# The order of work inside a step of the routed experts, on TensorE and on VectorE

## The reference, cut to what matters

```python
weights, indices = _gate(xt, gate_w)                 # 4 of 16 experts for each token
combine = jnp.einsum('tk,tke->te', weights, jax.nn.one_hot(indices, E, dtype=weights.dtype))
h1 = jnp.einsum('td,eid->tei', xt, W1)               # D = 256, inner width I = 176
h3 = jnp.einsum('td,eid->tei', xt, W3)
g = jax.nn.silu(h1) * h3 * combine[:, :, None]
y = jnp.einsum('tei,edi->td', g, W2)
```

## Time and profile before

| | us |
|---|---|
| median of 3 runs | 994.32 |
| the runs | 994.6, 990.09, 994.32 |
| the profiled execution | 992.58 |
| its span in the profile | 990.8 |

### The profile page before, as it was taken

One profiled execution on the slowest core, in us unless ns is written; L12 is line 12 of the kernel. 1 busy time (PEld: TensorE's weight loads), 2 busy tenths in 40 slices (PEclk: granted clock), 3 DMA queues, 4 the chain that ended last, 5 costly groups with the idle time before them and its releaser, 6 DMA issues.

```text
span 990.8 us, 19931 instructions
## 1 busy us (share of the span) xinstructions
PE 867.0 (88%) x6994; PEld 736.1 (74%) x6994; DVE 732.7 (74%) x1589; ACT 573.9 (58%) x1072; POOL 658.6 (66%) x625
## 2 busy tenths in 40 slices
PE   5688999999999999999999997738887899999940
PEld 5556777878878888788888786637775799999940
DVE  5777999987978788787888885585765466666648
ACT  1345777778887877887887886622321244444410
POOL 3555878978797888888788886515666555555530
PEclk9999999999999999999999999958997899999975
DMA  8661613223423235222325136233223333434337
GB/s 299 233 134 31 178 32 83 62 56 87 150 50 84 56 87 172 58 69 52 89 57 160 41 99 229 85 83 108 90 98 130 120 116 116 120 118 122 108 123 302
DMA packets 65757, 111.20 MB, mean 112 GB/s; under 512 B 16917, under 2 KB 43292, under 8 KB 63820
## 3 DMA queue, kind: packets, MB, share of 16 engines
q1 hardware_dynamic: 46905, 69.24, 26.4%
q10 hardware_dynamic: 11843, 22.84, 6.5%
q0 software_dynamic: 6912, 17.84, 4.9%
HBM read 46.06 MB, written 39.58 MB: 86 GB/s over the span
## 4 chain that ended last, share of the span: by engine, by line
PE 57%; DVE 11%; DMA 11%; POOL 11%; issue 5%; ACT 3%; SPq 0%; POOLq 0%; ACTq 0%; DVEq 0%
PE bank L691 12%; PE bank L693 10%; PE bank L692 10%; DMA slots<-h,slot_i 8%; PE bank L871 7%; PE bank L1087 7%; POOL p_lo L1927 5%; PE bank L848 4%; POOL turns L1905 2%; PE bank L1059 2%; PE bank L945 2%; DVE nmax L1261 2%; POOL slots L1983 1%; DVE qk L1241 1%; DVE turns L1235 1%
## 5 line engine op out<-in xcount | busy, mean ns | idle before, releaser
L1927 POOL TENSOR_TENSOR p_lo<-p_f,p_hi 128x512 f16<-128x512 f32 x256 | 329.5, 1299 | 46.2 <-ACT p_f L1662 45.2
L1659 ACT ACTIVATE p_hi<-bank,log_up 128x512 f16<-128x512 f32 x256 | 176.3, 689 | 108.0 <-PE bank L693 99.1
L1261 DVE TENSOR_REDUCE nmax<-bank 128x1 fp32r<-128x512 f32 x256 | 174.4, 685 | 84.4 <-PE bank L848 81.3
L1662 ACT ACTIVATE p_f<-bank,log_up 128x512 f32<-128x512 f32 x256 | 175.4, 685 | 14.7 <-POOL p_lo L1927 14.7
L871 PEld LDWEIGHTS bank<-vals,p_hi 128*128 128x128 f16 x2048 | 110.5, 98 | 59.2 <-POOL p_lo L1927 27.7
L871 PE MATMUL bank<-vals,p_hi 128*128 128x66 f16 x2048 | 138.8, 194 | 14.8 <-POOL p_lo L1927 14.5
L1905 POOL TENSOR_TENSOR turns<-turns 128x512 f32<-128x512 f32 x64 | 90.9, 1423 | 65.9 <-DVE turns L1235 65.9
L1241 DVE TENSOR_TENSOR qk<-rows_f,qk 128x512 fp32r<-128x512 f32 (+1 forms) x128 | 132.7, 1037 | 2.2
L691 PE MATMUL bank<-qk 128*128 128x512 f32 x256 | 122.2, 477 | 6.0 <-issue 4.8
L871 PE MATMUL bank<-vals,p_lo 128*128 128x66 f16 x1024 | 121.2, 193 | 0.0
L848 PE MATMUL bank<-qk 128*128 128x512 f32 x256 | 104.4, 411 | 3.6 <-DVE nmax L1261 3.2
(11 more groups left out here) (231 smaller groups left out, 2091.8 us busy)
## 6 DMA issues: line engine op xcount, KB each, us to landing
rows_f<-turns SPq DMA_DIRECT2D x64, 256.0 KB, 3.9
slots<-pad ACTq DMA_DIRECT2D x4, 2880.0 KB, 10.1
xs<-slots SPq DMA_DIRECT2D x80, 144.0 KB
w_hi<-parts SPq DMA_DIRECT2D x16, 512.0 KB, 8.4
rows_f<-kl_f SPq DMA_DIRECT2D x32, 192.0 KB, 3.0
w_raw<-in_w ACTq DMA_DIRECT2D x4, 1408.0 KB, 11.8
h_dram<-h_hl SPq DMA_DIRECT2D x3, 1024.0 KB, 4.9
qk<-lat_st SPq DMA_DIRECT2D x16, 192.0 KB, 4.3
```

What stands on the lines that cost most here:

```text
L1261: dve.tensor_reduce(nmax[:, k % MAXES:k % MAXES + 1], max_bank[q % 2][:], AX_X, ALU.max, negate=True)\
L1659: act.activation(p_hi[:, u % TB, :], score_bank[u % 2][:], ACT.Exp, bias=log_up[:, 0:1], scale=SCALE)
L1662: act.activation(p_f[:, u % 2, :], score_bank[u % 2][:], ACT.Exp, bias=log_up[:, 0:1], scale=SCALE)\
L1927: pool.tensor_tensor(p_lo[:, u % TB, :], p_f[:, u % 2, :], p_hi[:, u % TB, :], ALU.subtract).then_inc(s_pl, 1)
```

## The change

In TensorE's stream the transposes of tile n+3 move behind the first products of tile n+2. In VectorE's stream the copy to `gT` of tile n+1 moves ahead of the gated product and `sel_i` of tile n+2. No instruction is added or removed, and the semaphores that each waits for stay the same. ScalarE's, GpSimd's and SyncE's streams are unchanged.

```diff
@@ TensorE, expert_position @@
+                if within(n + 2, SLOT_TILES):
+                    m, par = n + 2, j % 2
+                    expert = experts[place + 2]
+                    pe.wait_ge(e_lo, m + 1)
...
+                    inner_products(par, par, ...).then_inc(e_h, 1)
                 if within(n + 3, SLOT_TILES):
...
                         mm = pe.transpose(x_bank[jm % 2][:, k * P:(k + 1) * P], xs[:, jm, k * P:(k + 1) * P], ident[:])
                     mm.then_inc(e_x, 1)
-                if within(n + 2, SLOT_TILES):
...
-                    inner_products(par, par, ...).then_inc(e_h, 1)
@@ VectorE, expert_position @@
+                if within(n + 1, SLOT_TILES):
...
+                    dve.tensor_copy(gT[:, par, 0].rearrange("p c t -> p (c t)"), g_bank[par][0:FC, 0:2 * P]).then_inc(e_gTc, 1)
                 if within(n + 2, SLOT_TILES):
...
                     dve.tensor_copy(sel_i[:, jm:jm + 1], sel[:, jm, 1:2]).then_inc(e_idx, 1)
-                if within(n + 1, SLOT_TILES):
...
-                    dve.tensor_copy(gT[:, par, 0].rearrange("p c t -> p (c t)"), g_bank[par][0:FC, 0:2 * P]).then_inc(e_gTc, 1)
```

More of the change, by code:

```diff
@@ L1050, in expert_position @@
                     place = j
+                if within(n + 2, SLOT_TILES):
+                    m, par = n + 2, j % 2
+                    expert = experts[place + 2]
+                    pe.wait_ge(e_lo, m + 1)
+                    if static(m) and m < 2:
+                        pe.wait_ge(z_g, 2 * NT)
+                    else:
+                        pe.wait_ge(e_g, m - 1)
+                    inner_products(par, par, lambda k: w_hi[:, bass.ds(expert, 1), k, :].rearrange("p a n -> p (a n)"),
+                                   lambda k: w_lo[:, bass.ds(expert, 1), k, :].rearrange("p a n -> p (a n)")).then_inc(e_h, 1)
                 if within(n + 3, SLOT_TILES):
@@ L1555, in expert_position @@
                     dve.tensor_reduce(sel[:, jm], chosen_by[:, jm], AX_X, ALU.add).then_inc(e_sel, 1)
+                if within(n + 1, SLOT_TILES):
+                    m, par = n + 1, (j + 1) % 2
+                    dve.wait_ge(e_gt, m + 1)
+                    if not (static(m) and m < 2):
+                        dve.wait_ge(e_y, m - 1)
+                    dve.tensor_copy(gT[:, par, 0].rearrange("p c t -> p (c t)"), g_bank[par][0:FC, 0:2 * P]).then_inc(e_gTc, 1)
                 if within(n + 2, SLOT_TILES):
```

## The result

| | before | after |
|---|---|---|
| median, us | 994.46 (6 runs) | 1011.75 (6 runs, 1009.74 to 1017.92) |
| profiled execution, us | 992.58 | 1009.74 |
| its span, us | 990.8 | 1007.9 |

The ratio of after to before is 1.0189, 95% interval 1.0165 to 1.0212. The changed kernel is slower by 17.3 us between the two medians, by about 19 us by the ratio (16 to 21 by its interval) and by 17.1 us between the two spans. The prediction was 1011.

A forecast was written before the change was run, and what follows sets the result against it. TensorE was taken to bound the routed experts' steps; a loop of 2.55 us replacing 2.268 gave +16.8 us, start's gain included, plus 1.0 for the low clock: +17.8, so 1010.4 or 1012.1, forecast 1011 us, range 1003 to 1025.

The forecast's parts named there:

- The loop and its length: Routed experts' steps: first products, next transposes, high half, low half, next first products close once a step, 2.55 us.
- 0.04: Loop term: from the transposes' end to the start of the high half on a free ScalarE, 0.04 us.
- 0.76: Loop term: from the low half's start to the first products that read it, 0.76 us, read at one place.
- The array's work: TensorE in the routed experts' steps needs 2.26 to 2.27 us a step of its own, whatever the order.
- VectorE's swap: Copy and gated product swapped on VectorE: nothing in the steady state; the start's gain alone would give -3.8 us.
- the low clock: After the start's idle time the clock is low and the loop longer there: +1.0 us, half of 2.
- The start: Tile 3's second products run in TensorE's idle time before 778.82; tile 6's products count from 779.1 us.
- the rival of the falling clock: Idle time of 0.28 us each step lowers the clock; such steps take 3.75 us, 1033 to about 1100; chance 0.08.
- The sequencer at every fourth step: Fetching the next tiles' experts every fourth step: put at 0; other end 0.2 us each time, 3.6 us, 1015.
- One sign: Middle steps: TensorE's busy share falls to about 89% at clock 1.00, about 0.28 us idle ahead of first product.

The follow-up runs named there:

- e4: Changed kernel with the next inputs' transposes moved behind those of the gated product, one place later still: 1026.59 us, 1.0333 of before, step 2.773 us.
- e6: Changed kernel with the high half copied in four activations of 64 columns instead of one of 256: 1023.53 us, 1.0307 of before, step 2.743 us.
- e3: Changed kernel with the two transposes put between the first three and last three first products: 991.12 us, 0.9983 of before, step 2.270 us.
- e5: Changed kernel with loads, transposes, high half and low half one tile further ahead: 991.20 us, 0.9970 of before, step 2.265 us.
- e2: Kernel before with VectorE's half of the change alone, TensorE in the old order: 990.18 us, 0.9969 of before, step 2.269 us.
- e1: Kernel before with TensorE's half of the change alone, VectorE in the old order: 1012.60 us, 1.0199 of before, step 2.555 us.
- e8: VectorE's half of the change alone, plus VectorE's conversion to `sel_i` two steps later, last in its step: 987.95 us, 0.9933 of before.

## Why the prediction was right

**The loop and its length: right, term by term.** The sum was 0.95 + 0.38 + 0.04 + 0.42 + 0.76 = 2.55. After reads 0.96 + 0.38 + 0.04 + 0.41 + 0.76 in the step shown, and 2.555 over 69 steps. The two terms that rested on the least held: 0.04, for which the row of a free ScalarE at the low clock was taken over the 0.09 of the steady step, and 0.76, which rested on one place. e4 and e6 show that the step follows the loop one for one (0.218 for 0.22, 0.188 for 0.19), e3 and e5 that it falls back to 2.27 as soon as the loop is shorter or spans another step.

**The array's work is the same in either order: right.** 2.265 to 2.270 in e2, e3 and e5, with three different orders.

**VectorE's swap costs nothing in the steady state and gains at the start: right, the gain smaller.** e2 shows both. Its gain is 3.1 us by the ratio and 1.4 in the traces, counted from the scatter's end (171.2 less 169.8). The forecast's own terms gave 3.8 for a kernel that has the start's gain and no loop, 2.8 with the low clock.

**The start: the mechanism right, its place in time off, the low clock too cheap.** The products of tile 6 were put at 779.1, 0.94 behind the conversion's start. After has them at 777.38 (the second one at 777.68, less the 0.30 spacing of the low clock), 0.99 behind the conversion at 776.39. What was off is the scatter's end itself, 1.8 us earlier than in the trace of before. The low clock was sized at +1.0, half of 2, because TensorE's idle time would be shorter; it was longer, 8.21 us. The low clock lasted from 777.23 to about 781.9 and cost 1.8: from 777.38 to the products of tile 79 at 965.67 it is 188.3, and 73 x 2.555 is 186.5. All of it falls in the first round, 4.37 us from the products of tile 6 to those of tile 7 (781.91 less 0.16). From the products of tile 79 on both kernels take the same, 42.2 and 42.3 us to the end of the span.

The price of such a round was also wrong in kind. The prediction took the loop at the low clock, 2.55 + 1.2 = 3.75, and so do the first steps of after, in which no second products run yet; they are 3.68 apart:

```profile
751.80 0.63 PE L1069 MATMUL bank<-ident,xs 128*128 128x128 f32 x2
...
755.48 0.63 PE L1069 MATMUL bank<-ident,xs 128*128 128x128 f32 x2
```

But in a full step at the low clock the array's own work is the longer one. In the old order, where nothing waits, such a step takes 4.33 (before, tiles 7 and 8):

```profile
780.67 0.64 PE L1059 MATMUL bank<-ident,xs 128*128 128x128 f32 x2
...
785.00 0.59 PE L1059 MATMUL bank<-ident,xs 128*128 128x128 f32 x2
```

So at that clock the new order costs next to nothing in a full step (4.37 and 4.33, one of each). A step of after at the low clock costs 1.8 over one at full clock, and not 1.2; the rival of the falling clock was priced a third too low.

**How near the number came is in part luck.** The products of tile 79 stand 17.15 us later than before (965.67 less 948.52). That is 73 x 0.287 = 20.95 for the longer steps, less 1.8 for the scatter's earlier end, less 2.0 for the rest of the start (the swap's gain and the low clock). The forecast had 20.6, nothing and 2.8 (3.8 less 1.0). The scatter's end moves from trace to trace and was not forecast; without it the difference of the two traces would have been 18.9.

**The sequencer at every fourth step: a few hundredths, not 0.2.** The idle time ahead of the waiting weight load runs 0.43, 0.43, 0.39, 0.45 and so on from step to step, with a pattern of four. All steps lie between 2.51 and 2.58.

**The clock: it stayed at 1.00.** The array stood for 0.28 us in each of 73 steps and the granted clock of 786 to 960 is 1.00. So the rule of the Trainium skill that the rival named ("TensorE: Matmul & The Clock Gate", "A second HAM failure mode: psum-queue depth-cycling") did not bite here, once the clock was full. In e4, with 0.5 us of standing time a step, the stretch from 800 to 940 us also has 1.00. These runs decide it, and not the shared expert's stretch, which the prediction held against the rival: its 0.94 hides two spells at 0.50, at its start and from 747 to 751, the second behind the 4.91 us shown above.

At the low clock the waits may matter, which the prediction did not have. The first steps of the routed experts run at 0.50 in every trace. In e2 the clock is at 0.50 from 750 to 755 and at 1.00 from 756 to 768. In after TensorE waits 1.09, 1.13 and 0.70 us at the head of the first three steps, and the clock stays low until about 761:

```profile
748.00:760.00 12.00, 8.95 (x31) 7.50 (x31) 2.91 (x14) 1.75 (x6) 7.67 (x9) 0.50 0.40 135
```

e1, e4 and e6 have such waits too and, like after, are low for about 14 us; the kernels with the short step, which wait less there, are low for about 7 (before for 3). That the waits held the clock down was not tested. Here it cost nothing, since TensorE stands for the scatter afterwards.

**One sign was wrong.** The prediction said that TensorE's busy share would fall to 89% in the profile. It reads 172.09 of 174, 99%. A matmul's row runs on for some time behind the point at which the next one could start (0.32 long, 0.16 apart), and these tails fill most of the standing time: in the step shown the second products' row ends at 863.36 (862.33 and 1.03), and the next first product's row starts at 863.39. So the idle time of 0.28 that the prediction looked for ahead of the first product cannot be read there either. It shows in the weight loads (0.43 ahead of L691) and in the number of matmuls in a microsecond, which fell to 89%. For the same reason the 160.00 of 160 us of the earlier trace rows did not by itself show that nothing waited before; what shows it is that the waits listed for that stretch of before have none of TensorE's weight loads among them.

## What to carry to other kernels

In a pipeline of steps that is bound by one engine, moving that engine's producer of a value from the front of a step to behind its consumer takes almost a step off the distance that hides the round trip. Before such a move, sum the round trip from start to start round the loop and compare it with the bound engine's own work in a step: the excess is paid each step (here to the hundredth of a microsecond), and a slack is worth nothing. A conversion that waits for a slow transfer should stand in its engine's queue as late as its reader allows, because all that stands behind it waits too.

## What the runs showed that had not been expected

- Standing time of the array hides in the busy share: 0.28 us of each 2.555 us step is 11%, and the profile's busy time shows 1%.
- From the low half's start to the weight load that waited for it, the traces of after and e1 show 0.61 to 0.68 us, of which 0.42 is VectorE's instruction. The 0.19 to 0.26 behind it include the address work that stands behind the wait.
- One activation of 256 columns takes 0.38 us, four of 64 columns in a row 0.57.
- The end of the first scatter to `parts` lies between 776.4 and 782.5 us in the traces of the eleven kernels, and TensorE stood 4.3 to 14.7 us for it. In before, that idle time was there and could be used; e8 did.
